# The tail of a fused attention and mixture-of-experts kernel: one expert slot beside each head group in the last batch, and the output projection among the four slots that follow

## The reference

```python
xn = layernorm(x)                                  # [4, 256, 512]
# attention: 32 heads of 16 features, 8 key/value groups of 4 heads each, causal
weights = softmax(where(causal, -inf, q @ k.T) / sqrt(16))
att = (weights @ v) @ Wo + bo
# experts: 16 routed ones, each token takes 4, and a shared one
z = silu(xn @ Wg[e].T) * (xn @ Wu[e].T) * cw[:, e]
ffn = sum_e z @ Wd[e].T + silu(xn @ Sg.T) * (xn @ Su.T) @ Sd.T
out = x + att + ffn
```

## Time and profile before

| | |
|---|---|
| median of 3 runs | 577.28 us (577.28 to 583.11) |
| the profiled execution: time | 577.56 us |
| its span | 575.7 us |
| PE busy | 466.4 us, 81% of the span |
| DVE busy | 372.6 us, 65% |
| ACT busy | 260.5 us, 45% |
| POOL busy | 258.7 us, 45% |
| last batch, from its first `scores` to the end of the span | 466.2 to 575.7 us |

### The profile page before, as it was taken

One profiled execution on the slowest core, in us unless ns is written; L12 is line 12 of the kernel. 1 busy time (PEld: TensorE's weight loads), 2 busy tenths in 40 slices (PEclk: granted clock), 3 DMA queues, 4 the chain that ended last, 5 costly groups with the idle time before them and its releaser, 6 DMA issues.

```text
span 575.7 us, 10261 instructions
## 1 busy us (share of the span) xinstructions
PE 466.4 (81%) x2984; PEld 344.4 (60%) x2984; DVE 372.6 (65%) x656; ACT 260.5 (45%) x385; POOL 258.7 (45%) x224
## 2 busy tenths in 40 slices
PE   0993669778998987989978779997888889889970
PEld 0882458556775765567756555775666557667640
DVE  7189975847885767268879872787764536766520
ACT  1441111146555454365577542656646335545610
POOL 3000392045554543365555863555567326464410
PEclk9996889969998998989999899999989999899986
DMA  7813943255575477665778964549655534424222
GB/s 281 323 46 81 235 177 111 92 190 173 100 140 167 75 143 221 111 160 99 145 236 208 273 139 68 148 116 213 205 110 98 103 56 75 74 44 88 38 38 36
DMA packets 32861, 78.25 MB, mean 136 GB/s; under 512 B 4320, under 2 KB 12000, under 8 KB 29600
## 3 DMA queue, kind: packets, MB, share of 16 engines
q0 software_dynamic: 11936, 27.53, 26.2%
q1 hardware_dynamic: 13904, 41.60, 22.2%
q10 hardware_dynamic: 6960, 8.39, 6.8%
HBM read 54.04 MB, written 23.33 MB: 134 GB/s over the span
## 4 chain that ended last, share of the span: by engine, by line
PE 49%; DVE 19%; issue 13%; ACTq 7%; ACT 6%; DMA 2%; POOL 2%; DVEq 1%; POOLq 0%; SPq 0%
PE psum L1047 27%; PE psum L1174 5%; DVE negm L867 3%; PE psum L1184 3%; PE psum L1140 3%; ACT wsplit L516 3%; PE psum L1008 3%; PE psum L1156 2%; PE psum L1071 2%; PE psum L1057 2%; ACTq L252 1%; ACTq L250 1%; DMA xn<-x 1%; PE psum L1076 1%; PE psum L1142 1%
## 5 line engine op out<-in xcount | busy, mean ns | idle before, releaser
L1047 PE MATMUL psum<-wsplit,xgT 128*128 (+1 forms) x660 | 178.8, 422 | 9.2 <-DVE xgT L752 9.2
L1047 PEld LDWEIGHTS psum<-wsplit,xgT 128*128 128x128 f32 x660 | 128.4, 201 | 38.2 <-issue 10.1
L421 POOL DMA_INDIRECT out<-ysb,tab x48 | 89.3, 1860 | 113.3 <-ACT ysb L549 99.5
L1047 PE MATMUL psum<-wsplit,zT 128*128 (+1 forms) x336 | 95.4, 421 | 20.1 <-DVE zT L859 20.1
L1047 PEld LDWEIGHTS psum<-wsplit,zT 128*128 128x128 f32 x336 | 62.3, 196 | 38.7 <-issue 27.0
L401 POOL DMA_INDIRECT xg<-xn_rows,tab x47 | 53.1, 1129 | 39.6 <-PE psum L1184 22.1
L503 ACT ACTIVATE th<-psum 128x256 f32<-128x256 f32 x55 | 21.2, 385 | 97.5 <-PE psum L1047 94.7
L426 POOL TENSOR_TENSOR wsplit<-wraw,wsplit (+1 forms) x16 | 40.1, 2507 | 54.2 <-ACT wsplit L516 51.9
L590 ACT ACTIVATE xn<-psum 128x1536 f32<-128x1536 f32 x32 | 46.4, 1450 | 37.0 <-PE psum L1142 37.0
L934 DVE TENSOR_TENSOR plo<-xn,phi 128x1536 f16<-128x1536 f32 x32 | 59.5, 1859 | 1.1 <-DVE ctxs L945 0.2
L907 DVE TENSOR_TENSOR xgT<-psum,xgT 128x512 fp32r<-128x512 f32 x47 | 32.3, 688 | 43.0 <-ACT xgT L512 40.9
(11 more groups left out here) (174 smaller groups left out, 637.5 us busy)
## 6 DMA issues: line engine op xcount, KB each, us to landing
wraw<-wexp SPq DMA_DIRECT2D x17, 1024.0 KB
wraw<-wexp SPq DMA_DIRECT2D x17, 512.0 KB, 4.5
q_parts<-stage ACTq DMA_DIRECT2D x12, 192.0 KB
q_pack<-q_parts ACTq DMA_DIRECT2D x6, 384.0 KB
xn<-x SPq DMA_DIRECT2D x4, 512.0 KB, 5.2
xn_rows<-xn SPq DMA_DIRECT2D x8, 256.0 KB, 7.7
ctxs<-x SPq DMA_DIRECT2D x8, 256.0 KB, 4.9
out<-ysb SPq DMA_DIRECT2D x8, 256.0 KB, 3.2
```

The lines of the kernel that those rows point to most:

```text
L421: nc.gpsimd.indirect_dma_start(out=out, out_offset=rows_of(s), in_=ysb[:, par, :], in_offset=None, compute_op=ALU.add).then_inc(y_out[par] ...
L1047: last = MM(dst, lhs(a, k), split_weights(place, w, c), start=m == 0, stop=m == len(products) - 1)
```

## The change

In the last batch the table `BESIDE` is replaced by `TAIL`. Head groups 0 to 6 have one slot each (slots 0 to 6), and group 7 has slots 7 to 11. The output projection no longer follows everything. The contexts are transposed in turn 9 (`CTX_AT`), the first half is projected at the end of turn 9 and the second at the start of turn 11. The two halves of `add_attention` become two DMAs of 256 KB (`add_half`), the first behind `add_rows` of turn 9 and the second behind that of turn 10; each waits for the landing of the scatter ahead of it, and the next scatter waits for the half. The last thing that POOL does is now the scatter of slot 10. In group 4 of the last batch `scores`, `numerators` and `high16` move behind `gate_up` and the tanh of slot 4, since the transposed maxima come only at the end of the turn of group 3. Batches 0 to 2 are as they were.

```diff
+TAIL = tuple((g,) for g in range(G - 1)) + (tuple(range(G - 1, SPS)),)
+CTX_AT = SPS - 3
...
 POOL, add_rows
+                if b == B - 1 and j > CTX_AT:
+                    pool.wait_ge(att_out, 16 * (B + j - CTX_AT))
...
+            def add_half(b, qt, s):
+
+                pool.wait_ge(att_sb, QT * b + (qt + 2))
+                pool.wait_ge(y_out[s % 2], 16 * ((s + 1) // 2 + 2))
+                pool.dma_start(out[T * b + qt * P:T * b + (qt + 1) * P, :], att[:, qt, :],
+                               accum_op=ALU.add).then_inc(att_out, 16)
...
                         add_rows(b, j)
-                add_attention(b)
+                        if last and CTX_AT <= j < CTX_AT + QT:
+                            add_half(b, j - CTX_AT, SPS * b + (j - 1))
+                if not last:
+                    add_attention(b)
...
-            pool.wait_ge(att_out, 16 * B + 16)
+            pool.wait_ge(att_out, 16 * B + 32)
+            pool.wait_ge(y_out[0], 8 * SPS * B + 16)
...
 ACT, sequence
+                    late = last and g == G // 2
+                    if not late:
+                        numerators(b, g)
...
                             tanh(s + U1, j % 2)
+                        if late:
+                            numerators(b, g)
...
+                        if last and j == CTX_AT:
+                            context_evac(b)
                         y_evac(b, j)
+                        if last and g == G // 2 - 1:
+                            minus_maxima(2 * b + 1, 1)
...
 DVE, sequence
+                        if last and j == CTX_AT:
+                            context(b, g)
+                        if last and j > CTX_AT:
+                            attention_half(b, j - CTX_AT - 1)
...
 PE, sequence
                             gate_up(j % 2, place)
+                        if late:
+                            scores(b, g, G * (b + 1))
...
+                        if last and j == CTX_AT:
+                            context_transposes(b)
+                        if last and j == SPS - 1:
+                            pe.wait_ge(nmT_sb, 2 * b + 2)
+                            project_out(b, 1)
                         pe.wait_ge(w_low[1], prev[1])
                         down(s + (U1 - 1), 1 - j % 2, prev[0])
...
+                        if last and g == G // 2 - 1:
+                            maxima_transpose(G * (b + 1), 1)
+                        if last and j == CTX_AT:
+                            project_out(b, 0)
```

More of the change, by code:

```diff
@@ L445, in sequence @@
                     causal(b, g)
-                    for j in BESIDE[g]:
+                    for j in (TAIL if last else BESIDE)[g]:
                         if not (last and j + 3 >= SPS - 1):
@@ L612, in sequence @@
                         high_part(QF * b + (B + QF + g), g, bank(3, T))
-                    for j in BESIDE[g]:
+                    for j in beside[g]:
                         s = SPS * b + j
                         slot_parts(s, 1 - j % 2, not (last and j + 1 >= SPS - 1))
-                        if j == BESIDE[g][-1] and (g == 3 or g == 7 and not last):
+                        if j == beside[g][-1] and not last and (g == 3 or g == 7):
                             minus_maxima(2 * b + (g // 4 + 1), 1 - g // 4)
@@ L619, in sequence @@
                             tanh(s + U1, j % 2)
-                        if j == BESIDE[g][0]:
+                        if late:
+                            numerators(b, g)
+                        if j == beside[g][0]:
                             high16(b, g)
-                        if j == BESIDE[g][0] and g < QF and not last:
+                        if j == beside[g][0] and g < QF and not last:
                             act.wait_ge(lo_done, QF * b + (B + QF + g + 1))
@@ L631, in sequence @@
                         act.wait_ge(parts_out[f], 16 * (b + 2))
-                context_evac(b)
+                    context_evac(b)
             for b in range(B):
@@ L949, in context, with attention_half @@
                 dve.wait_ge(ctx_done, i + 1)
-            def attention_out(b):
-                for qt in range(QT):
-                    dve.wait_ge(wo_ps, QT * b + qt + 1)
-                    if qt == 0:
-                        dve.wait_ge(att_out, 16 * b + 16)
-                    V.tensor_tensor(att[:, qt, :], bank(WO[qt]), bo_sb[:, :], ALU.add).then_inc(att_sb, 1)
+            def attention_half(b, qt):
+                dve.wait_ge(wo_ps, QT * b + qt + 1)
+                if qt == 0:
+                    dve.wait_ge(att_out, 16 * b + 16)
+                V.tensor_tensor(att[:, qt, :], bank(WO[qt]), bo_sb[:, :], ALU.add).then_inc(att_sb, 1)
             def sequence(b, last):
+                beside = TAIL if last else BESIDE
                 for g in range(G):
@@ L972, in sequence @@
                             low16(b, g)
-                    if g == G - 1:
+                    if g == G - 1 and not last:
                         context(b, g)
-                attention_out(b)
+                if not last:
+                    for qt in range(QT):
+                        attention_half(b, qt)
             gu_low(0, 1, 0)
@@ L1167, in output_projection, with project_out @@
                     last.then_inc(ct_ps, 1)
-                pe.wait_ge(nmT_sb, nm_count)
-                if b == 0:
-                    pe.wait_ge(wo_in, 16)
-                for qt in range(QT):
-                    pe.wait_ge(ct_sb, QT * b + qt + 1)
-                    for k in range(KD):
-                        last = MM(bank(WO[qt]), ctxT[:, qt, k, :], wo_sb[:, k, :], start=k == 0, stop=k == KD - 1)
-                    last.then_inc(wo_ps, 1)
+            def project_out(b, qt):
+                pe.wait_ge(ct_sb, QT * b + qt + 1)
+                for k in range(KD):
+                    last = MM(bank(WO[qt]), ctxT[:, qt, k, :], wo_sb[:, k, :], start=k == 0, stop=k == KD - 1)
+                last.then_inc(wo_ps, 1)
             def rows_transpose(s, par, count):
@@ L1199, in sequence @@
                 prev = expert_of(s0 - 1)
+                beside = TAIL if last else BESIDE
                 for g in range(G):
-                    scores(b, g, G * b + (min(g + 4, G) if last else g + 4))
+                    late = last and g == G // 2
+                    if not late:
+                        scores(b, g, G * b + (min(g + 4, G) if last else g + 4))
                     if g < QF and not last:
                         project(bank(3, T), T * (b + 1), g * P)
-                    for j in BESIDE[g]:
-                        s, first = s0 + j, j == BESIDE[g][0]
+                    for j in beside[g]:
+                        s, first = s0 + j, j == beside[g][0]
                         real = not (last and j == SPS - 1)
@@ L1230, in sequence @@
                                 weighted(b, g - 1)
-                        elif g == G - 1:
+                        elif g == G - 1 and j == beside[g][1]:
                             weighted(b, g)
+                        if last and g == G // 2 - 1:
+                            maxima_transpose(G * (b + 1), 1)
+                        if last and j == CTX_AT:
+                            project_out(b, 0)
                         if real:
                             prev = place, number
-                output_projection(b, 2 * b + (2 if last else 3))
+                if not last:
+                    context_transposes(b)
+                    pe.wait_ge(nmT_sb, 2 * b + 3)
+                    if b == 0:
+                        pe.wait_ge(wo_in, 16)
+                    for qt in range(QT):
+                        project_out(b, qt)
             for b in range(B):
```

10 lines of the change are left out of this document (5 added, 5 removed).

## The result

| | before | after |
|---|---|---|
| median | 577.28 us (576.14 to 583.11, 4 executions) | 586.05 us (585.22 to 586.87, 4 executions) |
| ratio to before, 95% interval | | 1.011 (1.006 to 1.016) |
| the profiled execution: time, span | 577.56, 575.7 us | 585.40, 583.6 us |
| last batch, first `scores` to the end of the span | 466.2 to 575.7: 109.5 us | 469.35 to 583.6: 114.2 us |

The changed kernel is about 1% slower, and the forecast of 574.9 us missed by 11 us, on the wrong side. Executions that are more than 1.5% above the fastest one of their kernel are left out of all ratios and means.

What follows compares the result with a forecast made beforehand. PE was taken to set the pace (81% busy), with a serial tail at the end. Gain 5.0 us (tail) - 1.8 (groups 0 to 4) - 0.5 (gaps) = 2.7 below the profiled 577.56, so 574.9 us; range 570 to 580.

Steps and rivals of the forecast that it cites:

- start of the last batch: First `scores` of the last batch, taken at 466.2 us from the trace of the kernel before.
- group 0: First one-slot turn of the last batch: 8.3 us, as `scores` of group 1 waits for DVE's `maxima`.
- groups 1 and 2: One-slot turns of the last batch: 7.5 us each, the length of such a turn in the trace of before.
- group 3 to the end of `gate_up` of slot 4: Last batch: 9.3 us with weight split, 0.75 for maxima split and transposes, 6.0 to the end, midway between clock cases.
- from there to `gate_up` of slot 6: Group 4's added waits: PE waits 2.7 us for the bank, POOL comes late; slot 6 starts 14.9 us after slot 4's `gate_up`.
- slots 6 to 9: Last batch up to the end of `gate_up` of slot 9: 22.2 us, 21.7 as before plus 0.5 for gaps.
- the tail: From the end of `gate_up` of slot 9 to the span's end: 31.2 us instead of 38.7, with DMAs ending the kernel.
- only about a third of the hidden projection returns as a queue: In the tail, 7.12 us of projection are hidden; about a third returns as five accumulating DMAs, none overlapping another.
- V: The end of `gate_up` of slot 9 in the last batch, forecast at 541.8 us.
- the quiet end: After the last DMA landing: a fixed 6.5 us with no traffic, whichever DMA lands last.
- long landings: Rival for the tail: half stores land nearly as late as whole ones, scatters cost more; 577.1 to 579.3 us, chance 0.20.
- POOL never catches up: Rival from group 4 on: POOL stays late, PE waits in turns 5 to 7, clock falls; 581.9 us, chance 0.12.

Runs made afterwards that it cites:

- free half stores: Changed kernel with both half stores sent to memory nobody reads, so neither they nor the scatters wait for each other; 579.7 us, ratio 0.9981 to the kernel before.
- the table alone: Changed kernel with the new table and group 4 order kept, but projection and one whole store at the end as before; 584.9 us, ratio 1.0091 to before.
- half of its table: Kernel before with one slot of the last batch taken from group 5 and given to the end; 573.8 us, ratio 0.9872 (576.1 us with two excluded executions).
- the best kernels: Reads moved and store split: on the kernel before, with `z_low` ahead of the last `low16`, 572.2 us (0.9836); on it with half the new table, 571.8 us (0.986).

## Why the prediction was wrong, by its own steps

Against the sum, the span ended 10.6 us late (583.6 for 573.0). By its terms, in the one profile of the changed kernel:

| term | sum | measured | difference |
|---|---|---|---|
| start of the last batch | 466.2 | 469.35 | +3.2 |
| group 0 | 8.3 | 8.4 | +0.1 |
| groups 1 and 2 | 7.5 each | 8.27, 8.42 | +1.7 |
| group 3 to the end of `gate_up` of slot 4 | 15.2 | 17.1 | +1.9 |
| from there to `gate_up` of slot 6 | 14.9 | 14.8 | -0.1 |
| slots 6 to 9 | 22.2 | 22.8 | +0.6 |
| the tail | 31.2 | 34.4 | +3.2 |

Two steps of the prediction failed: the 7.5 us for each of groups 1 and 2, and the statement that only about a third of the hidden projection returns as a queue.

- **Groups 1 and 2: the step "groups 1 and 2 take 7.5 each" failed**, and it is the failed term ahead of V that an experiment shows best. The row behind 7.5 is a turn in which the reads of the slot table stand behind `down` and `scores`; in the changed kernel they stand behind `weighted`. The prediction knew such gaps (0.5 us for four turns), and so undersized them: 7.0 us in the batch, where the two traces of before have 4.1 and 3.9. Moving the reads brought the turns back to 7.5 and the time down by 7.3 us, though nearly half of that is the clock of groups 3 and 4.
- **Group 3** lost by the same gap, 1.66 us ahead of the row transposes of slot 4 where the row of before has 0.65: PE had just waited 1.74 us for the split maxima, and its clock was low behind both. The stretch 507.0 to 511.5, `gate_up` of slot 4, has PEclk 0.62 in this table of stretches:

```profile
507.00:511.50 4.50, 4.50 (x16) 3.37 (x15) 1.14 (x3) 0.87 (x2) 0.00 (x0) 0.62 0.04 7
518.10:522.70 4.60, 4.59 (x15) 3.73 (x16) 1.32 (x3) 2.06 (x3) 4.45 (x4) 0.67 0.02 4
```

  The sum took the middle between a fallen clock and a full one; here it fell, and 1.0 us of the gap was missing besides. The conversion inside the split took 0.50 us, not 0.18 and not 2.36.
- **Group 4 was right** in its waits and its size. `high16` waits for POOL, and PE waits 2.31 us for ACT's copy (2.7 predicted):

```profile
515.05 1.48 ACT L611 ACTIVATE phi<-xn 128x1536 f16<-128x1536 f32 x1 [1.32 <-POOL xn L412]
```

```profile
518.11 0.69 PE L1087 MATMUL psum<-ident,zz 128*128 128x128 f32 x2 [2.31 <-ACT ysb L564]
```

  The clock fell behind this wait too (the second stretch above, 518.1 to 522.7, 0.67). POOL's lateness hides less of it than foreseen: ACT's copy ended at 525.71, 0.5 us before PE came to need it at 526.19, so it was PE that set the start of `gate_up` of slot 6.
- **The tail: the row of DMAs was foreseen, but the step "about a third of that returns as a queue" failed.** By the free half stores 5.7 of the 7.12 us returned, and by the table alone, whose tail with the projection at its end is 33.2 us, all of it. Much of the 38.7 of before was no projection but the wait and the slow `down` of slot 10, which the table takes away by itself.
- **The terms of its DMAs were too small.** The scatter of turn 9 starts at V + 3.3 as predicted, and the last one waits for the half store. But the steps from DMA to DMA are 5.03, 4.72, 5.21 and 4.70 us, 19.7 in all for 17.0 (4.7, 3.9, 4.5 and 3.9). A scatter takes 4.5 to 4.7 and not 4.2, a half 3.9 and not 3.7, and POOL starts a scatter 0.8 us after the half has landed, not 0.2. The rest is the end: 11.5 us from the last scatter's start for 10.9. The quiet stretch follows:

```profile
576.50:583.60 7.10, 0.00 (x0) 0.00 (x0) 0.00 (x0) 0.00 (x0) 0.00 (x0) 0.50 0.00 0
```

  It did not grow. Counted from the last packets, as here, it is 7.0 us in the trace of before (568.70 to 575.70) and 7.1 now. The sum took a scatter only to its last packets, at 4.2, and the quiet end from a landing 0.5 us behind them, at 6.5, and so lost that half microsecond between the two rows.

  The rival "long landings" had the right place and the wrong half: scatters in a row do cost more, a half does not land like a whole. The Trainium skill's rule (DMA: Bandwidth & Descriptors, anatomy of one DMA) takes only 0.6 us off for the second 256 KB, which is an estimate from its 436 GB/s, and that put the half at 5.3 us. The trace does not agree: 3.9 against 5.7 to 6.1 for the whole, so about 2 us for each 256 KB and 1.9 besides.
- **The start** was taken as fixed. It wanders by 7 us between kernels that do the same until there, and the profile of before was an early one. Nothing shows that part of the miss, 3.2 us, to be an effect of the change.
- **The balance of the change.** The sum had a gain of 5.0 in the tail against 1.8 and 0.5 lost. By the two profiles the tail gives 4.2 (38.7 to 34.4), and the part ahead of V takes 9.0 (70.9 to 79.8), 2.5 of them moved work. The table alone shows the same loss, so what the change does to the projection neither gains nor costs; the table costs, most of it ahead of slot 8, in the idle time of one-slot turns and in a lower clock. The slower rival, "POOL never catches up", did not happen: PE has one wait of over 1 us for the copy, not three.
- Open: how much of the loss is the reads, and why the clock fell in groups 3 and 4. Open too: how the 0.6% that is left with the reads moved is shared between group 3's wait for the maxima (2.3 us in that trace), the waits for ACT's copy (3.8 us) and the four turns at the end. Why the start wanders was not tried.

## What to carry to other kernels

Before compute is hidden behind a row of DMAs that accumulate into one tensor, count them as one serial queue, with the restart between landing and next issue (here 4.7 to 5.2 us a piece): the projection of 7 us was hidden, and at least 5.7 us of it came back as queue. When a turn's length is carried over from a trace, look at what stands ahead of each register read on PE in the old order and in the new one; here reads behind long matmuls cost next to nothing, and behind short ones each turn paid. Test the parts of a change alone: here half of its table costs nothing, the other half makes most of the loss, and the best kernels keep the projection at the end.

## What the runs showed of the hardware that was not expected

- Where two register reads stand behind short matmuls, PE is idle for 0.3 to 0.8 us, and once for 1.66 us, behind a wait. Moved ahead of six matmuls of 1.65 us together they leave two short waits, 1.1 us in all, in the last batch.
- After the waits and gaps of groups 3 and 4 the granted clock was 0.62 and 0.67, and with the reads moved 1.00; this is worth about as much as the idle time itself. What decides it was not tried.
- From the landing of one accumulating DMA to the start of the next on POOL's queue pass 0.55 us ahead of a direct one and 0.8 us ahead of an indirect one.
- A 256 KB accumulating store lands after 3.8 to 4.2 us, a 512 KB one after 5.7 to 6.2, once 7.1.
- The time from the start of the last DMA to the end of the span goes by its kind: 12.3 to 12.8 us for the whole store, 10.4 to 10.6 for a half, 11.1 to 11.5 for a scatter, though a scatter carries as many bytes as a half.
